# Six projection tiles of batch 0 computed in the last two recurrent steps instead of beside attention's first heads, and the first query tile of each batch behind its key tiles

## The reference

```
a = _layer_norm(audio_kv, ln_gamma, ln_beta)
Q = (hidden_states @ Wq.T).reshape(B, Tt, HEADS, HEAD_DIM).transpose(0, 2, 1, 3)
K = (a @ Wk.T).reshape(B, Ta, HEADS, HEAD_DIM).transpose(0, 2, 1, 3)
V = (a @ Wv.T).reshape(B, Ta, HEADS, HEAD_DIM).transpose(0, 2, 1, 3)
scores = jnp.einsum('bhtd,bhsd->bhts', Q, K) * scale
attn = jax.nn.softmax(scores, axis=-1)
out = jnp.einsum('bhts,bhsd->bhtd', attn, V)
return hidden_states + jnp.tanh(gate) * (out @ Wo.T)
```

## Time and profile before

| | |
|---|---|
| median of 3 runs | 3205.1 us (3204.63, 3205.1, 3209.02) |
| the profiled execution's own time | 3201.94 us |
| its span | 3200.2 us |
| attention, from the first score product to the end | 900.44 us of the span |
| PE busy, of the span | 3063.3 us |
| DVE, ACT, POOL busy | 2338.7, 1808.8, 226.9 us |
| mean granted PE clock | 0.986 of full |

### The profile page before, as it was taken

The page is one execution under the profiler, slowest core; times in us unless marked ns, Lnnn a source line. Parts: engine busy times, 40 slices in busy tenths (PEclk is TensorE's granted clock), DMA queues, the critical chain, the costliest instruction groups (busy, mean ns, idle before and its releaser), DMA issues.

```text
span 3200.2 us, 77104 instructions
## 1 busy us (share of the span) xinstructions
PE 3063.3 (96%) x32684; PEld 2287.3 (71%) x32684; DVE 2338.7 (73%) x3819; ACT 1808.8 (57%) x3311; POOL 226.9 (7%) x457
## 2 busy tenths in 40 slices
PE   6899999999999999999999999997998998998998
PEld 4667777777777777777777777775665665665666
DVE  3788788887888787887887788876377566566566
ACT  3556555565655555555556555555366556556555
POOL 0000000000000000000000000000110101111010
PEclk8889999999999999999999999998999999999999
DMA  3223333343333333344333333343334224234131
GB/s 132 65 89 126 126 107 127 108 153 132 126 126 126 126 105 129 108 148 137 126 119 133 122 104 129 107 174 116 106 80 108 56 66 108 65 84 104 41 80 41
DMA packets 110357, 349.41 MB, mean 109 GB/s; under 512 B 22848, under 2 KB 56256, under 8 KB 84032
## 3 DMA queue, kind: packets, MB, share of 16 engines
q0 software_dynamic: 39936, 234.91, 23.2%
q1 hardware_dynamic: 69648, 106.28, 10.5%
q10 hardware_dynamic: 432, 3.28, 0.3%
HBM read 252.11 MB, written 16.78 MB: 84 GB/s over the span
## 4 chain that ended last, share of the span: by engine, by line
PE 87%; DVE 7%; ACT 4%; issue 1%; DMA 1%; SPq 0%; ACTq 0%; DVEq 0%
PE psum L734 42%; PE psum L743 6%; PE psum L901 5%; PE psum L919 4%; PE psum L871 3%; PE psum L800 3%; PE psum L861 3%; PE psum L784 3%; PE psum L891 3%; DVE psum L1727 2%; PE psum L876 2%; PE psum L687 2%; PE psum L699 2%; PE psum L867 1%; PE psum L667 1%; DVE mem L1732 1%
## 5 line engine op out<-in xcount | busy, mean ns | idle before, releaser
L734 PE MATMUL psum<-rw 128*128 128x256 f32 x6144 | 1402.8, 384 | 9.0 <-DVE rw L1529 5.4
L734 PEld LDWEIGHTS psum<-rw 128*128 128x128 f32 x6144 | 1155.1, 191 | 218.9 <-issue 54.0
L1727 DVE CUSTOM_DVE_ANT_0 psum<-psum,mem 128x1024 f32<-128x1024 f32 x256 | 313.6, 1225 | 77.3 <-PE psum L891 77.2
L1271 ACT ACTIVATE rest<-psum,mem 128x1024 f32<-128x1024 f32 x256 | 285.1, 1114 | 89.5 <-DVE mem L1727 87.8
L1523 DVE SCALAR_TENSOR_TENSOR rw<-psum,rw 128x256 f32<-128x256 f32 x480 | 196.0, 475 | 144.8 <-PE psum L700 79.5
L1183 ACT ACTIVATE rw<-psum,own 128x256 f32<-128x256 f32 x384 | 214.5, 714 | 123.7 <-PE psum L784 123.5
L901 PE MATMUL psum<-ident,rest 128*128 128x128 f32 x2048 | 270.4, 275 | 2.7 <-DVE mem L1686 1.6
L1624 DVE TENSOR_TENSOR_SCAN rw<-rw 128x2112 f32<-128x2112 f32 x48 | 217.4, 4529 | 70.6 <-ACT rw L1176 69.1
L901 PEld LDWEIGHTS psum<-ident,rest 128*128 128x128 f32 x2048 | 235.2, 141 | 42.3 <-issue 14.7
L1919 POOL DMA_DIRECT2D rw<-big_dram x192 | 101.7, 531 | 2157.2 <-PE psum L734 2124.3
L1264 ACT ACTIVATE mem<-psum 128x512 f32<-128x512 f32 x256 | 152.1, 595 | 141.0 <-PE psum L901 141.0
(11 more groups left out here) (157 smaller groups left out, 4297.4 us busy)
## 6 DMA issues: line engine op xcount, KB each, us to landing
rw<-big_dram POOLq DMA_DIRECT2D x192, 1024.0 KB, 5.6
side<-mem POOLq DMA_DIRECT2D x256, 128.0 KB, 4.1
rw<-xs_dram SPq DMA_DIRECT2D x32, 512.0 KB, 3.8
side<-mem SPq DMA_DIRECT2D x256, 64.0 KB, 2.0
rw<-rw SPq DMA_DIRECT2D x192, 64.0 KB, 2.0
rw<-rw SPq DMA_DIRECT2D x384, 32.0 KB
xs_dram<-rw SPq DMA_DIRECT2D x24, 512.0 KB, 6.4
rw<-x_dram SPq DMA_DIRECT2D x16, 512.0 KB, 5.0
```

Source lines behind the costliest of these rows:

```text
L734: last = mm(t[:, o * TC:(o + 1) * TC], big[:, k, P * m:P * m + P], src[:, k, 0:TC], start=k == 0, stop=k == KT - 1, skip_group_check=True)
L1271: s_ring.empty(f(probs[:, n % HPT, :].rearrange("p (a s) -> p a s", a=2), s_ring.bank(n, "s"), ACT.Exp, scale=-1.0, bias=mx[:, n % 8:n % 8 ...
L1727: maxima.inc(nc.vector.tensor_tensor_reduce(t, t, mbias.rearrange("p (a s) -> p a s", a=2), 1.0, 3.4e38, ALU.add, ALU.min, accum_out=mx[:, ...
```

## The change

For batch 0, `v5`, `v6` and `v7` move from turns 0, 1 and 2 to step 24, behind `v4`; `k10`, `k11` and `q1` move from turns 4, 6 and 8 to step 25, behind the unit's last feed-forward tile; `q0` moves from step 23, where it stood between `var` and `rstd0`, to step 24, behind `k01`. For batches 1 to 3, whose first tiles are computed in the last turns of the batch before, `q0` moves from turn 48 to turn 55; their `v5` to `q1` stay in turns 0 to 8.

```
-          39: [(1, "sum0"), (1, "sum1")], 41: [(1, "mean0"), (1, "mean1")], 46: [(1, "var")], 48: [(1, "q0")], 50: [(1, "rstd0"), (1, "rstd1")], 53: [(1, "k00")], 54: [(1, "k01")],
+          39: [(1, "sum0"), (1, "sum1")], 41: [(1, "mean0"), (1, "mean1")], 46: [(1, "var")], 50: [(1, "rstd0"), (1, "rstd1")], 53: [(1, "k00")], 54: [(1, "k01")], 55: [(1, "q0")],
...
-FIRST = ["mean0", "mean1", "var", "q0", "rstd0", "rstd1", "k00", "k01"] + [f"v{n}" for n in range(5)]
+FIRST = ["mean0", "mean1", "var", "rstd0", "rstd1", "k00", "k01", "q0"] + [f"v{n}" for n in range(ST)] + ["k10", "k11", "q1"]
...
-    return [(b + off, name) for off, name in BESIDE.get(turn, ()) if 0 <= b + off < B]
+    return [(b + off, name) for off, name in BESIDE.get(turn, ()) if 0 <= b + off < B and (b + off or name not in FIRST)]
...
                 if s == ITS:
                     batch_tile(0, "k01")
+                    batch_tile(0, "q0")
...
                     batch_tile(0, "v4")
+                    batch_tile(0, "v5")
+                    batch_tile(0, "v6")
+                    batch_tile(0, "v7")
+                if s == ITS + 1:
+                    batch_tile(0, "k10")
+                    batch_tile(0, "k11")
+                    batch_tile(0, "q1")
...
                     batch_tile(0, "var")
-                    batch_tile(0, "q0")
                     batch_tile(0, "rstd0")
```

More of the change, by code:

```diff
@@ L70 @@
           16: [(0, "k20")], 18: [(0, "k21")], 22: [(0, "q2")], 26: [(-1, "wo2")], 30: [(-1, "wo3")], 32: [(0, "k30")], 34: [(0, "k31")], 38: [(0, "q3")],
[1 row of a table removed]
[1 row of a table added]
           56: [(1, "v0")], 58: [(1, "v1")], 60: [(1, "v2")], 61: [(1, "v3")], 62: [(1, "v4")]}
-FIRST = ["mean0", "mean1", "var", "q0", "rstd0", "rstd1", "k00", "k01"] + [f"v{n}" for n in range(5)]
-PARTS = ["q0", "k00", "k01"] + [f"{w}{e}{n}" for e in range(1, KT) for w, n in (("k", 0), ("k", 1), ("q", ""))]
+FIRST = ["mean0", "mean1", "var", "rstd0", "rstd1", "k00", "k01", "q0"] + [f"v{n}" for n in range(ST)] + ["k10", "k11", "q1"]
+PARTS = ["k00", "k01", "q0"] + [f"{w}{e}{n}" for e in range(1, KT) for w, n in (("k", 0), ("k", 1), ("q", ""))]
 def beside(n):
@@ L1336, in _ @@
                     after(0, "k01")
+                    after(0, "q0")
                 if has_b:
@@ L1402, in _ @@
                     after(0, "v4")
+                    after(0, "v5")
+                    after(0, "v6")
+                    after(0, "v7")
+                if s == ITS + 1:
+                    after(0, "k10")
+                    after(0, "k11")
+                    after(0, "q1")
                 if has_n:
@@ L1408, in _ @@
                     group_square(b, 1)
-                if s == ITS - 1:
-                    after(0, "q0")
                 if has_b:
```

## The result

The changed kernel takes 3216.39 us, median of 6 runs (3212.49 to 3221.06), against 3204.86 us for the kernel before in 6 runs beside them: a ratio of 1.0038 with a 95% interval of 1.0025 to 1.0052. That is 11.5 us slower; 12.5 were forecast.

The account below looks back on a forecast made before the run. PE, busy for 96% of the span, was taken as the bound, with turns without tiles bound by the PE, DVE and ACT round. Terms +1.6 + 10.4 + 10.1 - 15.5 + 1.1 + 4.8 = +12.5 us gave 3217.6 us, range 3206 to 3225.

Parts of the forecast that it names:

- q0 of batch 0: Steps 23 and 24: 3.48 us paid behind k01, 1.89 back from the shorter rstd0 chain; net +1.6 us.
- v5 to v7: Step 24 behind v4: three tiles at full cost, 3.48 us each, filling no hole; +10.4 us.
- k10, k11, q1: Step 25, ahead of first score product: +10.4 us, less 0.87 wait covered, +0.5 for the later first maximum; +10.1.
- Turns 0 to 11: Attention's start without six tiles: 38.59 us shrink to 23.1, bound by the round of two score buffers; gain 15.5 us.
- 1.1 for the clock: First turns of attention: PE idles more, so one loss at a lower granted clock was added, +1.1 us.
- the rival with 7.5 us: Clock falls and stays down over turns 0 to 7: 7.5 us in place of 1.1, total 3224.0 us; chance 0.10.
- q0 of batches 1 to 3: Turn 48 to 55: 3.48 us paid in turn 55, 1.9 back at turn 48; net +1.6 each, +4.8 in all.
- five waits in turns 48 to 54: PE's idling behind the next batch's layer norm and first key tile: 0.54, 0.96, 0.50, 1.31 and 2.08 us, 5.39 together.
- the rival of the free layer norm: Turns 48 to 54: with q0 gone the five waits vanish, -5.39 us per batch, 3196.6 us; chance 0.08.
- That the matmuls stay the same and PE is at 96%: Whole kernel, mere-shift rival: holes open at one place and close at another, sum about 0, 3205.1 us; chance 0.10.

Follow-up runs that it names:

- The filler: Changed kernel plus three matmuls with unread result behind turn 1's score product: 23.02 us from first score to second sum of values, against 23.56.
- the six tiles: Kernel before with only batch 0's v5 to v7, k10, k11 and q1 moved, q0 staying in all batches: ratio 1.0017.
- the values: Kernel before with only batch 0's v5 to v7 moved into step 24: 131.98 us from var to second sum of values, +5.6.
- the keys: Kernel before with only batch 0's k10, k11 and q1 moved into step 25: 126.50 us from var to second sum of values, +0.2.

## Why the prediction was right, step by step

*q0 of batch 0*: forecast +1.6, measured +2.3. The chain did shorten, `rstd0` starting as soon as the reciprocal was done (6.10 us after `var` for 7.44, forecast 1.48 less), but PE behind the wait ran at the lower clock and gave 0.8 us back. This term was sized without the clock. It also left out that `q0` waited for the load of the queries, for a time that differs by execution; against the other traces with the old order the term is 1.9 to 2.9.

*v5 to v7*: forecast +10.4, measured 10.26. They ran on without a hole behind `v4`. The run with `v4` moved shows why none of it was hidden: the wait for the unit's mixture was already covered by the tiles before.

*k10, k11, q1*: forecast +10.4 less 0.87 ahead of the first score, 9.5, measured 8.92. The record of a score product behind a tile starts 3.03 us after the tile (2321.73 against 2318.70), where the next tile comes 3.45 after, so 0.4 us of the difference seems to lie in how the start is recorded (the score product's own record is 1.02 us long there, and 0.70 where no tile stands ahead). The three together give 2.27 + 10.26 + 8.92 = 21.45, and the changed kernel shows 21.42.

*Turns 0 to 11*: forecast 15.5 won back, less 1.1 for the clock and 0.5 for the first maximum behind `q1`'s second part, 13.9; measured 14.1. The filler splits the two: the clock cost 0.54, half of the forecast. The forecast counts to the L919 of turn 11, which in the changed kernel starts 24.48 us behind the first score's record. At full clock that would be 23.9, and less the 0.4 of the record and the 0.5 of `q1`'s second part it is 23.0, for which the round of the two score buffers had given 23.1. (The first maximum starts 1.90 us after the score product, against 0.89 in the earlier trace rows: the same 0.4 and 0.5, and 0.1.) The granted clock was 0.89 over turns 0 to 7, so it did not stay down, as the rival with 7.5 us had it.

*q0 of batches 1 to 3*: forecast +1.6 each, measured +1.76 each. 2.08 came back at turn 48 (1.9 forecast), and 3.84 were paid from turn 55 to 59 (18.20 us for 14.36; 3.48 forecast). PE has a gap of 0.3 us ahead of `v0` there, whose bank is now the one that `q0` had.

The sum of the terms as measured is 7.3 + 5.3 = 12.6 us, against 12.5. The median moved by 11.5; its interval, 8 to 17 us, holds both. That the sum fits better than its terms is in part luck. The two terms of `q0` came out 1.2 us larger than forecast, and those of the six tiles 1.0 us smaller. And the lower clock at `k01`, 1.70 us each time, which the prediction has nowhere, fell in two of three batches in the profiled execution before and in two of three after, so that it cancels in the difference. The prediction also counts five waits in turns 48 to 54 and leaves out a sixth, 0.32 us ahead of the score product of turn 53; only the rival of the free layer norm rests on that sum. That the matmuls stay the same and PE is at 96% was no reason for an unchanged time, and the free layer norm did not come about: ACT's affine part and the bank of `k00` hold these waits, as the run with `q0` in turn 52 and the one with `v0` in turn 53 show from two sides.

## What to carry to other kernels

A tile of work costs its own length less the hole that it fills, so ask of the place that it leaves what it covered there, and of the new one whether the bound engine is idle at all. Where independent work fills the first rounds of a pipeline that has yet to start, leave it there: ahead of the pipeline it costs its full length, and the empty rounds give back less (`v5` to `v7` cost 5.6 us net; `k10`, `k11` and `q1` cost 0.1 to 0.2 while turns 0 to 2 kept their tiles). A hole in one engine is best filled with work whose buffer the late engine need not free: `q0` in turn 52, which ACT had to round behind its long work, opened a wait of 3.87 us, and `v0` in turn 53 closed one of 2.08. Find what the wait is on, and put there what needs only what is already done.

## What the runs showed of the hardware

The same wait of 2.06 to 2.08 us ahead of `k01` was followed by a fall of the granted clock in some passes and not in others. Counted in the eight traces that keep this wait (the kernel before, the changed one, and the runs with the six tiles, q0 in turn 55, q0 of batch 0, the values, the keys, and the filler), it fell in 12 of 24 passes. It then cost 1.70 us each time: `k01` takes 5.40 us (5.38 once) and not 3.70, at a granted clock of 0.65 in place of 1.00 (the second and the first batch before). So two traces of one kernel can differ by up to 5.1 us in these three places alone, and single passes have to be compared at the same clock; I had put the clock's cost at the new first turns only. Other waits of these traces stand on either side: behind the 1.31 us ahead of `k00` it fell in none of 24 passes, behind 1.24 us ahead of `k01` (`q0` in turn 51) in none of 3, behind 3.87 us (`q0` in turn 52) in 3 of 3, behind 2.46 us in step 23 in 3 of 3 traces. Why it falls in one pass and not in the next, no run here shows.
